# First attention of a two-layer kernel: one stream over all turns, scores as stacked fp32r products, another distance between scores and transposes

## The chip, the cores and the metric

One NeuronCore of a Trainium2 chip. The metric is the device time of one launch in microseconds (us), the median of the runs. Names: TensorE is PE in the profile, VectorE is DVE, ScalarE is ACT, GpSimd is POOL, and SP is the SyncE queue that issues most of the transfers.

## The reference, cut to what matters

Two layers over 8 sequences of 256 tokens with 256 features. Each is LayerNorm, an attention, a mixture of experts as a gate, and a residual. The change is in the attention of layer 0:

```python
q = heads(hidden_states @ wq.T + bq)      # 32 heads of 8 features
k = heads(hidden_states @ wk.T + bk)
v = heads(hidden_states @ wv.T + bv)
scores = jnp.einsum('bhqd,bhkd->bhqk', q, k) / np.sqrt(HD).astype(np.float32)
scores = jnp.where(causal, scores, -jnp.inf)
attn = jax.nn.softmax(scores, axis=-1)
out = jnp.einsum('bhqk,bhkd->bhqd', attn, v)
return out.transpose(0, 2, 1, 3).reshape(B, S, H) @ wo.T + bo
```

Beside it runs the router of layer 0: `xn @ Wr.T`, a softmax over 8 experts and the best two of each token. After it come the experts' blocks, then layer 1.

## The kernel before, in words

**Turns and slots.** The first attention goes over four turns of 512 tokens, two sequences each (TURNS, CH). A turn has 32 slots (SLOTS), 16 for each of its two sequences (PAIRS, the index bb). A slot is one pair of heads of one sequence; `pair_of` gives its sequence, the half mt of the features, j, and the two groups of 32 partitions in which its heads lie.

**A slot.** `scores` (L624 to L630) makes the causal blocks of 256 queries against 256 keys of both heads, 384 columns a head, one PSUM bank each: an fp32 product of 256 columns (L624), one of 128 (L626), and a bf16 product that adds the mask (L630). Slots alternate between banks 0, 1 and 2, 3, so the scores of slot s wait until the exponentials of s-2 have read them. The keys lie four times in SBUF (`kTm`), each copy masked to one head in four, so that a head is picked out of 32 partitions by zeros. DVE takes the maxima of both heads (L839, L841), ACT the exponentials with their sums (L742, L744), TensorE transposes them (`turn`, L640, three blocks a head, into banks 4 and 5), DVE copies them to SBUF (`copy_probs`, L780), and once in two slots `pv` (L659, L662) multiplies four heads by the values, into bank 6 or 7.

**The order** is written out by hand, one program for each engine, with semaphores. TensorE: scores(s), what stands beside (`beside`), transposes of s-2, and pv. DVE: maxima of s, copies of s-2, beside. ACT: exponentials of s, beside. So LAG = 2 on both TensorE and DVE. Beside the slots run the values (L561), the router's products (L568), the bias row (L575) and the turning of the next turn's normalised tokens (L246), and on DVE the statistics and scaling of the next turn (L216, L226) and the routing (from L357; the ranks are read at L450, the slots finished at L478).

**Between two turns** stand the transposes of the inverse sums (`turn_inverse`, L673), the normalising on DVE (L793), queries and keys of the next turn (`pe_queries_keys`, L550; ACT L710 for queries, DVE L772 for the masked keys, four writes each), and the output projection (`project`, L684) with its DVE add (L799). The scores of a turn start once its queries and keys are ready, at slot 0 (the wait is in `scores`).

**Queues.** SP loads the inputs, constants and all of x, then the first pair's weights of layer 1 (`load_pair(0)`), the shared and routed experts of layer 0, then writes zeros to the rows in DRAM to which tokens are scattered (L2132, eight transfers of up to 2 MB). POOL has the variances of each turn (`pool_all`), then, in the last turn, one scatter of tokens a slot (L502). Once all is scattered, SP loads the first blocks (L2138) and `pe_blocks0` begins (L881).

Of the kernel before, what the change touches and what calls it, by code (L numbers as in the profile page):

```python
# [19 lines left out]
F32 = mybir.dt.float32  # L20
# [24 lines left out]
RING = 3  # L45
LAG = 2
# [57 lines left out]
def build(nc, A, out, phases=3):  # L104
    with ExitStack() as ctx:
# [63 lines left out]
        MASK = cols[:, 0:4]  # L169
        G_NORM = cols[:, 12:13]  # L170
        BQ, BK, BV, BO = (cols[:, 4 + 2 * i:6 + 2 * i] for i in range(4))
# [89 lines left out]
        kTm = carve("attention", HPQ, KC, CH)  # L261
        qT = carve("attention", KC, CH)
# [3 lines left out]
        inv_wide = carve("attention", 2, ST * NH0, HD0)  # L266
        nmax = carve("attention", RING, ST, 2)
        total = carve("attention", 2, ST, NH0)
        inv0 = carve("attention", 2, ST * NH0)
        BLOCKS_AT = SPLIT1 + 2 * 512 + 32  # L270
        assert BLOCKS_AT > 2 * KC * CH + HPQ * KC * CH
# [25 lines left out]
        q_done, k_done, v_done = count("q_done", KC), count("k_done", KC), count("v_done", 2)  # L297
        qT_ready, v_ready = count("qT_ready", KC), count("v_ready", 2 * HPQ)
        keys_ready = count("keys_ready", KC * HPQ)
# [215 lines left out]
        ZERO_PARTS = -(-NB0 // TILES) - (-NB1 // TILES)  # L515
# [10 lines left out]
        ln_stats, ln_mean, ln_rstd = (carve("stay", *n) for n in ((2, 6), (TILES, 2), (TILES, 2)))  # L526
# [7 lines left out]
        def pair_of(s):  # L534

            w = s % PAIRS
            return s // PAIRS, w // (PAIRS // 2), (w % (PAIRS // 2)) // 2, (2 * (w % 2), 2 * (w % 2) + 1)

        def head_of(n):
            bb, mt, j, rows = pair_of(n // 2)  # L540
            return mt * (NH0 // KC) + rows[n % 2] * HPQ + j

        def pe_queries_keys(pe, t, mt):

            xT = norm0.xT
            if mt == 0:
                pe.wait_ge(norm0.xT_ready.sem, norm0.xT_ready.at(t, KC))
            for which, bank, done in ((0, 2 + mt, q_done), (1, 4 + mt, k_done)):
# [3 lines left out]
                last.then_inc(done.sem, 1)  # L552

        def pe_attention0(pe, t):
            xT = norm0.xT
            rows7 = ps[:, 7, :]
# [8 lines left out]
            def logits(turn):  # L565
                for c in range(CT):
                    for kc in range(KC):
                        last = pe.matmul(rows7[:, c * E0:(c + 1) * E0], xT[:, kc, c * P:(c + 1) * P], router0[:, kc, :],  # L568
                                         start=kc == 0, stop=kc == KC - 1)
# [8 lines left out]
            def beside(s):  # L578
# [1909 lines left out]
```

## Time and profile before

| what | value |
|---|---|
| median of 3 runs | 1947.15 us (1938.78 to 1947.18) |
| the profiled execution's own time | 1924.45 us |
| its span | 1922.6 us |
| PE, DVE, ACT, POOL busy | 94%, 67%, 47%, 43% |
| mean granted clock | 0.983 |
| first attention, first scores to the first block's product | 27.1 to 418.8 us |
| chain that ended last, by engine | PE 77%, DVE 10%, POOL 5% |

Busy time is the time in which an engine has an instruction in flight. A timeline row merges neighbouring instructions of one line: its duration reaches to the end of the last, some 0.15 to 0.25 us of which overlaps with the next row on PE. So the distance between starts is what a step costs in the stream. A matmul of fp32 leaves two records.

### The profile page before, as it was taken

How to read it: one execution, taken by the hardware profiler on the slowest of the kernel's cores; microseconds unless marked ns; L12 is line 12 of the kernel's file. 1: busy time of each engine (PE TensorE's matmuls, PEld its weight loads, DVE VectorE, ACT ScalarE, POOL GpSimd, SP SyncE). 2: the span in 40 equal slices, each digit the busy share in tenths (PEclk: the TensorE clock that was granted, in tenths of full speed). 3: DMA queues.
4: the chain of work that ended last, by engine and by line, in shares of the span. 5: the costliest groups of instructions: out<-in, count | busy, mean ns of one | idle time of the engine just before them, and what ended most of it. 6: DMA issues, size and time to landing. Idle time of an engine off the chain costs nothing.

```text
span 1922.6 us, 34586 instructions
## 1 busy us (share of the span) xinstructions
PE 1815.3 (94%) x11822; PEld 1443.5 (75%) x11822; DVE 1282.4 (67%) x2811; ACT 906.2 (47%) x2978; POOL 832.7 (43%) x919
## 2 busy tenths in 40 slices
PE   6999999999987999999999999999999997999986
PEld 4767666767765887788888888888888886777754
DVE  5678787863457788888676766667667664444467
ACT  3657564753433444445454455544545543444422
POOL 2000000320056665565767767777676773000066
PEclk9899999999999999999999999999999998999999
DMA  9600000123342000000000000000000223333344
GB/s 345 231 1 2 1 1 1 59 90 112 90 158 94 1 1 12 1 6 1 15 20 14 19 16 14 19 14 11 25 11 22 77 78 136 106 108 107 105 132 123
DMA packets 75907, 114.29 MB, mean 59 GB/s; under 512 B 9505, under 2 KB 65953, under 8 KB 73089
## 3 DMA queue, kind: packets, MB, share of 16 engines
q1 hardware_dynamic: 66416, 86.38, 13.6%
q0 software_dynamic: 9216, 25.18, 4.0%
q8 instruction: 75, 1.23, 0.3%
q10 hardware_dynamic: 144, 1.05, 0.1%
q14 instruction: 56, 0.45, 0.1%
HBM read 64.86 MB, written 47.71 MB: 59 GB/s over the span
## 4 chain that ended last, share of the span: by engine, by line
PE 77%; DVE 10%; POOL 5%; issue 3%; ACT 3%; DMA 2%; POOLq 0%; DVEq 0%; SPq 0%; ACTq 0%
PE ps L1356 11%; PE ps L1371 9%; PE ps L1443 5%; PE ps L1889 5%; PE ps L1397 4%; PE ps L640 4%; PE ps L624 3%; PE ps L1385 3%; PE ps L1384 3%; PE ps L1383 3%; PE ps L902 2%; POOL work L2084 2%; PE ps L1378 2%; PE ps L1906 2%; PE ps L1908 2%
## 5 line engine op out<-in xcount | busy, mean ns | idle before, releaser
L1356 PE MATMUL ps<-work,weights 128*128 128x256 f32 x1024 | 248.3, 386 | 1.1 <-DVE work L1629 1.1
L1371 PE MATMUL ps<-split 128*128 128x512 f32 x768 | 227.8, 419 | 0.0
L1356 PEld LDWEIGHTS ps<-work,weights 128*128 128x128 f32 x1024 | 186.4, 191 | 22.1 <-DVE work L1629 1.3
L1771 POOL TENSOR_TENSOR work<-work,rope 128x512 f32<-128x512 f32 x128 | 164.5, 1286 | 53.1 <-ACT work L1544 53.0
L1777 POOL TENSOR_TENSOR work<-work 128x512 f32<-128x512 f32 x128 | 164.4, 1284 | 5.0
L502 POOL DMA_INDIRECT xg<-work x96 | 96.9, 1009 | 153.1 <-PE ps L630 140.2
L2084 POOL DMA_INDIRECT work<-yg,work x64 | 62.4, 975 | 227.1 <-DMA yg<-work 207.3
L742 ACT ACTIVATE work<-ps,work 128x128 f32<-128x128 f32 x256 | 95.4, 373 | 124.3 <-DVE work L841 117.4
L1371 PEld LDWEIGHTS ps<-split 128*128 128x128 f32 x768 | 130.9, 190 | 24.6
L780 DVE COPY work<-ps 128x384 f32<-128x384 f32 x256 | 130.0, 549 | 8.5 <-PE ps L640 8.4
L1443 PE MATMUL ps<-weights,work 128*128 128x256 f32 x512 | 124.0, 386 | 2.5 <-ACT work L1600 2.5
L640 PE MATMUL ps<-ident,work 128*128 128x128 f32 x768 | 116.5, 283 | 8.1 <-DVE work L780 8.0
L1651 DVE TENSOR_TENSOR work<-ps,keep_w 128x384 f32<-128x384 f32 x128 | 65.4, 553 | 87.1 <-PE ps L1379 86.8
L744 ACT ACTIVATE work<-ps,work 128x256 f32<-128x256 f32 x256 | 122.4, 478 | 0.0
L2021 DVE SCALAR_TENSOR_TENSOR work<-work,ps 128x176 f32<-128x176 f32 (+1 forms) x95 | 35.0, 369 | 121.5 <-ACT work L1972 121.5
L1585 ACT ACTIVATE work<-ps,work 128x128 f32<-128x128 f32 x256 | 90.6, 366 | 51.4 <-PE ps L1385 51.1
L1443 PEld LDWEIGHTS ps<-weights,work 128*128 128x128 f32 x512 | 99.4, 195 | 16.8 <-ACT work L1600 3.1
L1664 DVE RECIPROCAL work<-ps 128x256 f32<-128x256 f32 x64 | 111.9, 1748 | 0.0
L1550 ACT COPY work<-ps 128x256 f32<-128x256 f32 x128 | 47.1, 368 | 130.3 <-PE ps L1371 130.3
L1889 PE MATMUL ps<-weights,work 128*128 x316 | 106.8, 461 | 0.2 <-ACT work L1966 0.2
L1383 PE MATMUL ps<-work 128*128 128x64 f32 (+1 forms) x512 | 97.3, 272 | 9.1 <-DVE work L1651 9.1
L640 PEld LDWEIGHTS ps<-ident,work 128*128 128x128 f32 x768 | 88.1, 145 | 22.8 <-issue 11.5
(236 smaller groups left out, 4508.8 us busy)
## 6 DMA issues: line engine op xcount, KB each, us to landing
work<-xg SPq DMA_DIRECT2D x118, 128.0 KB, 2.2
yg<-work SPq DMA_DIRECT2D x118, 128.0 KB, 1.7
xg<-work SPq DMA_DIRECT2D x6, 2048.0 KB, 17.8
weights<-in_w SPq DMA_DIRECT2D x8, 1024.0 KB, 9.4
weights<-in_f SPq DMA_DIRECT2D x8, 1024.0 KB, 5.1
weights<-in_f SPq DMA_DIRECT2D x1, 4864.0 KB, 16.0
work<-xn SPq DMA_DIRECT2D x32, 128.0 KB, 2.2
weights<-in_wo SPq DMA_DIRECT2D x1, 2048.0 KB, 8.6
```

What stands on the lines that cost most here:

```text
L640: last = pe.transpose(ps[:, 4 + hh, k * P:(k + 1) * P], prob[:, s % RING, hh, k * P:(k + 1) * P], ident[:, :])
L744: act.activation(pr[:, P:BLK], sc[:, 0:SEQ], ACT.Exp, bias=nmax[:, s % RING, 1, hh:hh + 1], accum_out=total[:, bb, 1, h:h + 1]).then_inc(e ...
L780: dve.tensor_copy(probT[:, s % RINGT, hh, :], ps[:, 4 + hh, 0:BLK]).then_inc(probT_ready.sem, 1)
L1356: last = pe.matmul(ps[:, 2, which * SEQ:(which + 1) * SEQ], w1(h, (which * KC + kc) * P, P), xT[:, kc, :], start=kc == 0, stop=kc == KC - 1)
L1371: last = pe.matmul(ps[:, 3, :], x1_split[:, xp, kc, c * P:(c + 1) * P], w_vg[:, n % 2, wp, kc, :], start=i == 0, stop=i == KC * len(TERMS) ...
L1383: pe.matmul(outs[0], left[:, 0:P], rhs[0], start=True, stop=True)
L1443: last = pe.matmul(ps[:, 7, c * D:(c + 1) * D], ogT[:, hh, c * P:(c + 1) * P], weights[:, W1O + h * D:W1O + (h + 1) * D], start=h == 0 and ...
L1664: dve.reciprocal(enz[:, n % 2, :, :].rearrange("p c n -> p (c n)"), ps[:, 0, SEQ:2 * SEQ])\
L1771: pool.tensor_tensor(qk[:, h % 4, :, :], raw[:, h % 2, :, :], rope[:, 0, :].unsqueeze(1).broadcast_to([P, 2, SEQ]), ALU.mult).then_inc(rot ...
L1777: pool.tensor_tensor(qk[:, h % 4, :, :], qk[:, h % 4, :, :], rot_s[:, h % 2, :, :], ALU.add)\
L1889: last = pe.matmul(ps[:, 2 + b % 2, 0:GUW], xb4T[:, b % 2, kc * P:(kc + 1) * P], experts1[:, bass.ds(offset[b] + kc * GUW, GUW)], start=kc ...
L2084: pool.indirect_dma_start(out=yk4[:, c % 2, k, :], out_offset=None, in_=yg1[:, :], in_offset=bass.IndirectOffsetOnAxis(ap=route1.index[:, ...
```

## The change

- **One stream.** The four turns become one run of 128 slots (ALL), numbered g. What stood between the turns stands beside the slots: inverses and output projection of the first sequence at slots 22 and 24, of the second at 6 and 8 of the next turn; the four projections of the next turn at 16, 18 (18, 20 in the routed turn), 28 and 30; values at 10 and 26. All these are even slots; pv stands in odd ones.
- **Distances.** `LAG, BACK = 3, 2`: TensorE transposes g-3 in slot g, DVE copies g-2 in slot g. The ring of exponentials grows to 4.
- **Stacked scores.** Queries and keys are split into an fp32r upper part and the rest (`split_heads`, on DVE for turn 0, on POOL for the others) and written to DRAM with SP's queue (`write_halves`, 4 transfers of 256 KB a projection); from there stacks of 32 partitions a head are loaded (`load_stack`, 256 KB for two slots, a ring of 5): every pair of halves (a, b) of 8 features. One fp32r product over 32 partitions then gives the whole score. The masked keys (L772) go; weights wq and wk are laid out by heads on the host.
- **SP's order.** The zeros go in 15 parts between stack loads, the experts' weights in parts in turn 2, then the shared ones and the first pair.
- **Routing.** Its DVE steps are spread over more slots; ranks and slots are worked out at slots 2 and 4 of turn 3.

The diff, cut to its core:

```diff
-RING = 3
-LAG = 2
+RING = 4
+LAG, BACK = 3, 2
+FIRST = 16, 18
+ALL = TURNS * SLOTS
+RINGQ = 5
...
+        def split_heads(eng, t, n):
...
+            eng.wait_ge(full_ready.sem, full_ready.at(t, n + 1))
+            if index >= 2:
+                eng.wait_ge(halves_written[ring], 16 * 4 * (index // 2))
+            eng.tensor_copy(halves[:, ring, 0, :], full[:, ring, :]).then_inc(upper_ready.sem, 1)
+            eng.wait_ge(upper_ready.sem, upper_ready.at(t, n + 1))
+            eng.tensor_tensor(halves[:, ring, 1, :], full[:, ring, :], halves[:, ring, 0, :], ALU.subtract).then_inc(lower_ready.sem, 1)
...
+            def lower_bank(t, s):
+                if s == 0 and 0 < t < TURNS - 1:
+                    pe.wait_ge(full_ready.sem, full_ready.at(t, PROJ))
+                    logits(6)
+                if s == 2 and t == TURNS - 1:
...
+                    route0.pe_rank(pe, 6)
+                if s == 22 and t < TURNS:
+                    turn_inverse(t, 0)
+                if s == 24 and t < TURNS:
+                    project(t, 0)
+                if t < TURNS - 1:
+                    if s == 26:
+                        pe.wait_ge(s0_ready.sem, s0_ready.at(t, 1))
+                        values(0)
+                    if s == 28:
...
+                        heads(t + 1, 2, 6)
+                    if s == 30:
...
+                        heads(t + 1, 3, 6)
...
             def scores(g):
...
+                if g % 2 == 0:
+                    pe.wait_ge(stack_loaded[n % RINGQ], 16 * (n // RINGQ + 1))
+                if g >= 2:
+                    pe.wait_ge(exp_done.sem, exp_done.at(0, 2 * g - 2))
+                heads = [(2 * (g % 2) + hh, stack[32 * r:32 * r + 32, n % RINGQ, 0, :], stack[32 * r:32 * r + 32, n % RINGQ, 1, :])
...
+            for g in range(ALL + 9):
+                t, s = divmod(g, SLOTS)
+                if g < ALL:
+                    scores(g)
+                lower_bank(t, s)
+                upper_bank(t, s)
                 for hh in range(2):
-                    if LAG <= s < SLOTS + LAG:
-                        turn(s - LAG, hh)
-                if s > LAG and (s - LAG) % 2 == 0:
-                    pv(s - LAG - 2)
-            turn_inverse(0)
...
-                pe_queries_keys(pe, t + 1, 1)
-            project(0)
-            project(1)
+                    if LAG <= g < ALL + LAG:
+                        turn(g - LAG, hh)
+                if LAG < g <= ALL + LAG and (g - LAG) % 2 == 0:
+                    pv(g - LAG - 2)
...
+            for g in range(ALL + 9):
+                if g < ALL:
+                    largest(g)
+                if BACK <= g < ALL + BACK:
+                    copy_probs(g - BACK)
+                beside(*divmod(g, SLOTS))
...
+            def load_stack(n):
...
+                for w in range(2):
+                    sp.wait_ge(halves_written[w], 16 * 4 * (t * KC + mt + 1))
+                if n >= RINGQ:
+                    sp.wait_ge(scores_done.sem, scores_done.at(0, 4 * (n - RINGQ) + 4))
...
+            for n in range(PROJ):
+                write_halves(0, n)
+                if n == 1:
+                    for i in range(HPQ):
+                        load_stack(i)
+            for i in range(HPQ, RINGQ):
+                load_stack(i)
+            for n in range(RINGQ, TURNS * STACKS):
+                t, i = divmod(n, STACKS)
+                if t < TURNS - 1 and i == 14:
+                    write_halves(t + 1, 0)
+                    write_halves(t + 1, 1)
+                if t and i == HPQ:
+                    write_halves(t, 2)
+                    write_halves(t, 3)
+                load_stack(n)
+                if 0 <= n - RINGQ - 2 < ZERO_PARTS:
+                    zero_rows(n - RINGQ - 2)
+                if t == 2 and i < E0:
+                    load_expert(i)
```

## Rows read from the trace of the kernel before

**Rows 1.** The page's row of busy times, whole span.
```profile
PE 1815.3 (94%) x11822; PEld 1443.5 (75%) x11822; DVE 1282.4 (67%) x2811; ACT 906.2 (47%) x2978; POOL 832.7 (43%) x919
```

**Rows 2.** Windows: us; PE, PEld, DVE, ACT, POOL busy; PEclk; DMA share; GB/s.
```profile
27.10:38.90 11.80, 11.42 (x87) 9.32 (x88) 9.91 (x24) 7.58 (x39) 1.22 (x2) 1.00 0.97 384
38.90:52.60 13.70, 13.70 (x84) 9.65 (x84) 8.02 (x18) 5.43 (x26) 0.00 (x0) 0.50 1.08 380
133.80:230.00 96.20, 92.02 (x855) 66.21 (x856) 75.09 (x158) 59.69 (x271) 1.21 (x2) 1.00 0.01 2
```

**Rows 3.** Timeline of TensorE, 84 to 96: start, us, engine, line, operation, count.
```profile
87.57 0.70 PE L624 MATMUL ps<-work 32*128 32x256 f32 x4
88.66 0.82 PE L640 MATMUL ps<-ident,work 128*128 128x128 f32 x6
91.43 0.64 PE L659 MATMUL ps<-work,weights 128*32 128x256 f32 x8
92.21 0.70 PE L624 MATMUL ps<-work 32*128 32x256 f32 x4
```

**Rows 4.** Timeline of DVE, same stretch.
```profile
88.89 0.42 DVE L839 TENSOR_REDUCE work<-ps 128x2 f32<-128x256 f32 x1
89.82 1.01 DVE L780 COPY work<-ps 128x384 f32<-128x384 f32 x2
90.75 0.42 DVE L839 TENSOR_REDUCE work<-ps 128x2 f32<-128x256 f32 x1
```

**Rows 5.** Timeline of ACT, same stretch.
```profile
90.00 0.37 ACT L742 ACTIVATE work<-ps,work 128x128 f32<-128x128 f32 x1 [1.06 <-DVE work L841]
```

**Rows 6.** Timeline of all engines, 114 to 150.
```profile
118.22 0.98 PE L640 MATMUL ps<-ident,work 128*128 128x128 f32 x6 [1.02 <-DVE work L780]
118.78 1.02 DVE L780 COPY work<-ps 128x384 f32<-128x384 f32 x2 [0.24 <-PE ps L640]
138.48 0.37 ACT L742 ACTIVATE work<-ps,work 128x128 f32<-128x128 f32 x1 [9.01 <-DVE work L841]
140.26 0.70 PE L624 MATMUL ps<-work 32*128 32x256 f32 x4 [0.53 <-ACT work L744]
```

**Rows 7.** Timeline of TensorE, 640.5 to 644: fp32r products of the second attention.
```profile
642.56 0.48 PE L1340 MATMUL ps<-split,tri_r 128*128 128x256 f32 x2
642.87 0.33 PE L1343 MATMUL ps<-split,ones_r 128*128 128x128 f32 x2
```

**Rows 8.** Timeline, 114 to 150: products between two turns.
```profile
122.99 3.60 PE L550 MATMUL ps<-work,weights 128*128 128x512 f32 x8
130.30 3.62 PE L684 MATMUL ps<-weights,work 128*128 128x256 f32 x16
```

**Rows 9.** Timeline, 0 to 48: products beside the first slots.
```profile
28.20 1.89 PE L561 MATMUL ps<-weights,work 128*128 128x256 f32 x8
36.29 1.85 PE L568 MATMUL ps<-router,work 128*128 128x8 f32 x16
```

**Rows 10.** Timeline: first projection read, first and last scores, first block.
```profile
22.07 0.69 ACT L710 ACTIVATE work<-ps,bqs 128x512 f32<-128x512 f32 x1 [2.75 <-PE ps L550]
27.11 0.70 PE L624 MATMUL ps<-work 32*128 32x256 f32 x4
...
406.65 0.70 PE L624 MATMUL ps<-work 32*128 32x256 f32 x4
418.83 0.60 PE L881 MATMUL ps<-ident,work 128*128 128x128 f32 x4
```

**Rows 11.** DMA issues: 256 KB from SBUF to DRAM, last number us to landing.
```profile
xn<-work SPq DMA_DIRECT2D x8, 256.0 KB, 2.1
```

**Rows 12.** Timeline of DVE: statistics, then first and last of twelve slot steps.
```profile
139.29 1.40 DVE L216 BATCH_NORM_STATS2 work<-x_res 128x6 f32<-128x256 f32 x4
...
296.57 0.29 DVE L450 COPY work<-ps 128x136 f32<-128x136 f32 x1
299.85 0.18 DVE L478 CAST work<-work 128x32 int32<-128x32 f32 x1
```

More of the change, by code:

```diff
@@ L257, in build @@
         eps_row, eps_dk, zeros = minus_half[:, 16:32], minus_half[:, 32:32 + ST * 2], minus_half[:, 48:49]
-        kTm = carve("attention", HPQ, KC, CH)
-        qT = carve("attention", KC, CH)
+        stack = part(0, RINGQ, 2, SEQ)
+        halves = part(RINGQ * 2 * SEQ, 2, 2, CH)
+        FULL_AT = RINGQ * 2 * SEQ + 4 * CH
+        full = work[:, FULL_AT:FULL_AT + 2 * CH].rearrange("p (a n) -> p a n", a=2)
+        assert FULL_AT + 2 * CH <= SPLIT1
+        used["attention"] = SPLIT1
         oT0 = carve("attention", KC, CH)
@@ new lines, in act_heads, with act_attention0, values @@
+        def act_heads(act, t, n, bank):
+            which, mt = n % 2, n // 2
+            index = t * PROJ + n
+            act.wait_ge(proj_done.sem, proj_done.at(t, n + 1))
+            if index >= 2:
+                act.wait_ge(lower_ready.sem, lower_ready.at(0, index - 1))
+            act.activation(full[:, n % 2, :], ps[:, bank, :], ACT.Identity, bias=(bqs, BK)[which][:, mt:mt + 1],
+                           scale=(HD0 ** -0.5, 1.0)[which]).then_inc(full_ready.sem, 1)
+        def act_attention0(act):
+            def values(t, c):
@@ new lines, in act_attention0, with dve_attention0, copy_probs, inverse @@
+            values(0, 0)
+            for g in range(ALL + 5):
+                if g < ALL:
+                    exponentials(g)
+                beside(*divmod(g, SLOTS))
+        def dve_attention0(dve):
+            def copy_probs(g):
+                for hh in range(2):
+                    dve.wait_ge(prob_turned.sem, prob_turned.at(0, 2 * g + hh + 1))
+                    if g >= RINGT:
+                        dve.wait_ge(pv_done.sem, pv_done.at(0, 2 * (g - RINGT) + hh + 1))
+                    dve.tensor_copy(probT[:, g % RINGT, hh, :], ps[:, 4 + hh, 0:BLK]).then_inc(probT_ready.sem, 1)
+            def inverse(t, bb):
@@ new lines, in _, with zero_rows, load_expert @@
+            zeros_to = [(rows, b0, min(b0 + ZB, blocks)) for rows, blocks in ((xg0, NB0), (xg1, NB1)) for b0 in range(0, blocks, ZB)]
+            def zero_rows(n):
+                if n == 0:
+                    sp.wait_ge(s_zeroed, 1)
+                rows, b0, b1 = zeros_to[n]
+                sp.dma_start(rows[b0 * P:b1 * P, :].rearrange("(b p) d -> p b d", p=P), S[:, ZB:ZB + b1 - b0, :])\
+                  .then_inc(xg_zeroed, 16)
+            def load_expert(e):
+                if e == 0:
+                    sp.wait_ge(s2_lower, 1)
+                    sp.wait_ge(bias_done, 6)
+                at = W0F + e * EW
+                sp.dma_start(weights[:, at:at + EW], A["f0"][:, e * EW:(e + 1) * EW]).then_inc(f0_loaded, 16)
@@ L2230, in _ @@
                 norm0.pool_all(pool, t)
+                for n in range(PROJ):
+                    split_heads(pool, t, n)
             pool.wait_ge(xg_zeroed, 16 * ZERO_PARTS)
@@ L2269, in _ @@
             dve.tensor_copy(bias_wide, BV.unsqueeze(2).broadcast_to([P, KC, P])).then_inc(bias_ready0, 1)
+            for n in range(PROJ):
+                split_heads(dve, 0, n)
             dve.wait_ge(consts_loaded, NCONST)
```

493 lines of the change are left out of this document (244 added, 249 removed).

## Prediction

> **What bounds the kernel now.** I read the page first: TensorE is busy 94% of the span [rows 1]. Then I cut the span into stages with the view of windows. The change touches only what runs from the start to the last projection of the first attention, some 420 of 1922.6 us; in a whole turn (133.8 to 230.0) TensorE is busy 92 of 96 us, DVE 75, ACT 60 [rows 2]. Third, the timelines of single engines inside a turn, because the busy share doesn't say who waits for whom. Two slots take 4.64 us on TensorE (87.57 to 92.21) with no gap: scores and masks 1.09 (87.57 to 88.66), the six transposes 0.75 to 0.9, and once in two slots the product by values, 0.78 (91.43 to 92.21) [rows 3]. So the slot, 2.32 us, is TensorE's own work. DVE needs 1.86 for a slot: 0.93 for the two maxima (88.89 to 89.82) and 0.93 for the two copies (to 90.75) [rows 4].
>
> **The new score products.** An fp32 product leaves two records of two passes; before, a slot has 4 records of 256 columns and 4 of 128. With fp32r it has 2 and 2, one pass each. The rows have fp32r products of 256 columns every 0.155 us (two in 642.56 to 642.87), so there is no fourfold pass left [rows 7]. The two heads run side by side in different rows of the array. From two passes twice to one pass once, 256 and 128 columns at 2.4 GHz, 0.48 us goes, and 0.61 is left from the first score product to the first transpose. Upper bound 1.09 (nothing gained), lower bound 0.35 (masks and one weight load); I take 0.61, next to the 0.67 that the fp32r row would give.
>
> **The new order, which is the point.** In slot g TensorE now issues scores(g), then what stands beside, then the transposes of g-3. DVE in slot g does the maxima of g, then the copies of g-2. So the copies that DVE does in its slot g-1 are those of g-3, and their transposes stand behind scores(g) on TensorE. Scores(g) have to wait for the exponentials of g-2, whose two PSUM banks they reuse. That closes a loop of two slots, and each hop has a row:
> - maxima start to exponentials start: 1.11 (88.89 to 90.00) [rows 4, 5];
> - exponentials start to the next scores in those banks: 1.78 (138.48 to 140.26) [rows 6];
> - scores to transposes: 0.61;
> - transposes to the first copy: 0.56 (118.22 to 118.78) [rows 6];
> - two copies, then the maxima of g: 0.93 [rows 4].
> Sum 4.99 us for two slots, 2.50 for one, against 2.32 now. Before, transposes of s-2 stood in slot s on both engines, so the same loop took three slots: with the old scores 5.47/3 = 1.82, hidden under TensorE's 2.32. The change takes 0.48 us from TensorE per slot (its own work would be about 1.84), and puts a wait in its place: TensorE idles some 0.65 and DVE some 0.63 in each slot. From the first scores (27.11) to those of slot 127 (406.65) it is 379.5 us now [rows 10]. After, 63.5 pairs x 4.99 = 317.
>
> **What stands beside, on TensorE.** It stands between scores(g) and the transposes, so inside the loop, and always in even slots, so always in the same of the two interleaved chains: nothing of it falls into the idle time. A projection of 512 columns costs 1.8 (8 records, two calls, 3.60) and an output projection 1.8 (16 records, two calls, 3.62) [rows 8]; the four transposes of an inverse 0.5, as four of a slot's six (0.82 with their tail) [rows 3]; half the values 1.8 (1.89), the router's products 1.8 (1.85) [rows 9]. Turn 0: router 1.8, bias row 0.9, values 1.8, turning x 1.0 (as the inverses, twice), four projections 7.2, inverse 0.5, output 1.8, values of the next 1.8: 16.8. Turn 1: the same without bias, with the inverse and output left from turn 0: 18.2. Turn 2: once more the router, 20.0. Turn 3: ranking (no row alone; 0.7, of little weight), two inverses, two outputs, one values: 7.1. Sum 62.
>
> **Beside, on DVE.** Steps in odd slots lengthen the same chain: statistics and scaling at slots 3 and 7, 1.4 each [rows 12], three turns, 8.4; eleven small routing steps in odd slots of turn 2 at 0.29 (twelve take 3.46, 296.57 to 300.03) [rows 12], 3.2. In even slots they fall on the other chain, which has 4.99 - 2 x 1.86 = 1.27 to spare: inverses (1.0), normalising and output copies (0.7) are hidden there, and would cost up to 19 us in all (two of each a turn) if the loop were shorter. The slots' computation in slot 2 of turn 3, 3.5 behind an inverse of 1.0, sticks out by 3.2. Sum 14.8. Gone are the masked keys, eight DVE writes a turn between the turns.
>
> So first to last scores: 317 + 62 + 14.8 = 394, 14 more than now. The seams between turns, where the old kernel drains, are worth little, since they are filled with projections (122.99 and 130.30 in [rows 8]): in a turn of 96 us, 32 slots x 2.32 = 74, beside 6.7, and the seam's products 11.6 leave 3.7 of waiting.
>
> **Start, end, and what moves to other queues.** The first scores wait for a way through DRAM: projection, ACT, two DVE steps (the first projection is there at 22.07 [rows 10]; ACT 0.7 and two DVE steps of some 0.6 bring it to about 24.0), four writes of 256 KB on SP's queue, the same for the keys, then a load of 256 KB. A transfer of this size takes 2.1 us to land [rows 11], the engines moved 384 GB/s [rows 2], so 2 MB need 5.5: halves there at about 30.3, first stack at 32.9, first scores at 33.0 instead of 27.11. +6 (bounds +3, if the writes overlap wholly, and +12, if each waits in turn). Later writes and stacks (16 MB each way over 400 us, 80 GB/s) have four stacks, 20 us, of lead: free; if not, a load is 2 to 5 us on the path of a stack. The zeros, weights of the experts and of the first pair leave the first 75 us and go out between stack loads; they are needed after turn 2 or later: free. POOL splits 12 projections, two steps each, where it idled: free. The end: now 12.2 us from the last scores to the first product of the blocks (406.65 to 418.83) [rows 10]; after, half the inverse and output work is already done, but the chain scores, maxima, exponentials, transposes, copies, values, output remains: -1.
>
> **The clock.** In turn 0 it is granted at 1.2 GHz from 38.9 to 52.6, after 11.8 us with the router's 8-column products and gaps, though TensorE counted as busy for 11.4 of them [rows 2]. The changed kernel idles before the first scores and in every slot, and issues the router's products four times in the stream. I add 6 us (estimate; bounds 0 and, as a rival, far more).
>
> Sum: +14 + 6 - 1 + 6 = **+25 us**. The profiled execution took 1924.45 around a span of 1922.6, 22.7 under the median 1947.15; +25 makes it 1949.5, and the median, against which I predict, 1972. With 0.35 or 1.09 for the scores the pairs give -17 or +30 on that; with the other bounds the forecast's own range is +8 to +45. About 0.5%, 9.7 us, is what a measurement can tell from no change.
>
> **Rivals.**
> 1. *The loop is shorter than I say, and the change is faster.* If copies of g-2 don't have to wait behind scores(g+1), the slot is bounded by work: DVE 1.87, TensorE 1.84, and products beside fall partly into idle time. Then 128 x 1.87 + 62 + 15 = 316, times 1.04 for waits like those at the seams, 329 instead of 380: with the start, -45 us, 1902. A weaker form: the slot is 2.50, but half of the 62 us hides: 1941. It decides from a slot period under 2.3 on. For it: before, TensorE alone set the pace, so no row shows my loop binding. Against: each hop is a semaphore wait in the code, with a row for its length. 0.27, the weak form 0.05 of it.
> 2. *The clock falls for long.* TensorE's work per slot sinks by a fifth and its period grows, with a gap in every slot, and in turn 0 the clock fell behind a stretch with gaps. At 1.2 GHz two old slots cost between 7.8 (84 records in 13.7 us, 24 to a slot [rows 2]) and 9.3 (twice 4.64); less 2 x 0.96 for the scores 5.9 to 7.4, say 6.2. If half the stage runs so: 32 pairs x 1.2, and 31 us of the beside work a second time: +69 on the forecast, 2041. Against: in turn 1 the granted clock was 1.00 over 96 us with gaps at the seam [rows 2]. The Trainium skill, TensorE: Matmul & The Clock Gate, section Part 4: PE-mode transpose, says that transposes do not count as busy in the way other matmuls do; six of them make up a third of a slot now and would make up as much after, with the score products shorter; by that rule this case comes true, with 2041. Turn 1's row speaks against it, with the same transposes at full clock, and no run yet shows the changed mix. 0.10.
> 3. *Cancelled.* Loop as forecast, but start, clock and part of the beside work cheaper, 1947 within 10 us. 0.10.
>
> **How the numbers follow.** Forecast 0.53. Faster by over 0.5%: rival 1 without its weak form, 0.22. Within 0.5%: the weak form and rival 3, 0.15. Slower: forecast and rival 2, 0.63. Range 1918 to 2015: it holds the forecast with its bounds (0.53), rival 3 and the weak form (0.15), the milder halves of rival 1 (a partly shorter loop) and of rival 2 (0.11 and 0.05), some 0.84 before allowing for what I have not thought of; left out are rival 1 in full and a clock down for half of the stage.
>
> **What would show it.** Right: in a plain stretch maxima every 2.50 us; DVE idle about 0.6 before the copies, released by the transposes; TensorE idle before the first score product, released by ACT; score groups about 0.6 long; first scores at about 33; a turn of about 100 us. Wrong: a period under 2.3, DVE idle at the maxima instead of the copies, products beside that don't lengthen their slot, or windows with a granted clock near 0.5 in turns 1 to 3.

## The result, and the profile after

The changed kernel takes 2010.68 us (median of 4 runs, 2010.25 to 2016.34); the kernel before takes 1944.04 on the same chip (4 runs, 1938.78 to 1947.18). The ratio is 1.035 (95% interval 1.032 to 1.039): 66.6 us slower. The prediction was slower by 25, with 1918 to 2015 as its range. The sign is right, and so are the loop that was forecast and most terms, but more than half of the loss is missing.

The page of the changed kernel, with the groups that answer to [rows 1] and to the steps of the sum:

```profile
PE 1790.1 (89%) x11310; PEld 1425.4 (71%) x11310; DVE 1268.3 (63%) x2787; ACT 906.5 (45%) x2986; POOL 855.8 (43%) x943
...
q8 instruction: 107, 1.75, 0.4%
...
L827 DVE COPY work<-ps 128x384 f32<-128x384 f32 x256 | 131.8, 552 | 135.8 <-PE ps L705 130.0
...
L810 ACT ACTIVATE work<-ps,work 128x128 f32<-128x128 f32 x256 | 95.4, 373 | 182.5 <-DVE work L907 169.4
...
L689 PE MATMUL ps<-split 32*128 32x256 f32 x256 | 53.0, 404 | 101.3 <-ACT work L812 93.4
...
L705 PE MATMUL ps<-ident,work 128*128 128x128 f32 x768 | 116.5, 291 | 0.7 <-DVE work L827 0.7
```

The three waits of the forecast loop are among the costliest: DVE's copies (L827) wait for the transposes (L705), ACT's exponentials (L810) for the maxima (L907), and TensorE's scores (L689) for the exponentials (L812). The transposes hardly wait for the copies, 0.7 us in all. TensorE did less (1790 us busy against 1815) in more time.

Where the stage's time lies, by the timeline of the changed kernel: first and last maxima, and the first product of the blocks.

```profile
36.99 0.42 DVE L905 TENSOR_REDUCE work<-ps 128x2 f32<-128x256 f32 x1 [2.17 <-PE ps L695]
...
452.66 0.41 DVE L905 TENSOR_REDUCE work<-ps 128x2 f32<-128x256 f32 x1
...
464.36 0.85 PE L937 MATMUL ps<-ident,work 128*128 128x128 f32 x3
```

First and last maxima of the kernel before:

```profile
30.11 0.41 DVE L839 TENSOR_REDUCE work<-ps 128x2 f32<-128x256 f32 x1
...
407.93 0.42 DVE L839 TENSOR_REDUCE work<-ps 128x2 f32<-128x256 f32 x1 [0.81 <-PE ps L630]
```

The first product of the blocks stands at 418.83 there [rows 10]. So the start costs 6.9 us more, the stream takes 415.7 where it took 377.8, and the end 11.7 for 10.9. Together 45.5 us are lost by the first product of the blocks. Another 20 are lost in a part that the diff doesn't touch, the second attention (experiments on TensorE's places).

The two profiles lie further apart than the medians, 86.2 us (spans of 2008.8 and 1922.6), and the rest of it isn't the change's. From the last product of L1951 (L1889 in the kernel before) to the end, the changed kernel's profile takes 119.3 us and that of the kernel before 101.4. Both lengths occur whatever the kernel: 100 to 102 us in the profiles of the first four experiments and of three later ones, 115 to 121 in four, among them the kernel before with nothing but waits added (116.5). Of each chip with more than one profile, all showed the same of the two. What decides between them stays open; a ratio of two kernels on one chip should be free of it.

**The loop, hop by hop.** Timeline of the changed kernel in a plain pair of slots, DVE, ACT and TensorE:

```profile
402.01 1.02 DVE L827 COPY work<-ps 128x384 f32<-128x384 f32 x2 [1.23 <-PE ps L705]
...
402.95 0.41 DVE L905 TENSOR_REDUCE work<-ps 128x2 f32<-128x256 f32 x1
403.06 0.38 PE L689 MATMUL ps<-split 32*128 32x256 f32 x2 [0.76 <-ACT work L812]
...
403.66 0.82 PE L705 MATMUL ps<-ident,work 128*128 128x128 f32 x6
...
404.05 0.37 ACT L810 ACTIVATE work<-ps,work 128x128 f32<-128x128 f32 x1 [1.05 <-DVE work L907]
404.19 1.02 DVE L827 COPY work<-ps 128x384 f32<-128x384 f32 x2 [0.23 <-issue]
...
405.92 0.39 PE L689 MATMUL ps<-split 32*128 32x256 f32 x2 [0.65 <-ACT work L812]
...
406.52 0.82 PE L705 MATMUL ps<-ident,work 128*128 128x128 f32 x6
```

Maxima to exponentials 1.10 (402.95 to 404.05), exponentials to the next scores in those banks 1.87 (to 405.92), scores to transposes 0.60 (to 406.52), transposes to copies 0.53 (403.66 to 404.19), copies to maxima 0.94 (402.01 to 402.95): 5.04 us for two slots. Forecast were 1.11, 1.78, 0.61, 0.56 and 0.93, 4.99 in all.

**A pair with a product beside.** Timeline of TensorE in the changed kernel, turn 3, with an output projection (L612, two calls):

```profile
387.33 0.39 PE L689 MATMUL ps<-split 32*128 32x256 f32 x2 [1.43 <-ACT work L812]
...
387.94 1.89 PE L612 MATMUL ps<-weights,work 128*128 128x256 f32 x8
389.67 0.82 PE L705 MATMUL ps<-ident,work 128*128 128x128 f32 x6
...
394.11 0.38 PE L689 MATMUL ps<-split 32*128 32x256 f32 x2 [1.44 <-ACT work L812]
```

From 387.33 to 394.11 are 6.78 us, 5.04 and the 1.73 of the product (387.94 to 389.67). TensorE stands still for 1.43 us before the scores in the same pair, and the product does not go there, since its place in the order is inside the loop.

**The clock.** Windows by turn (columns as in [rows 2]), first the changed kernel, then turn 0 of the kernel before:

```profile
37.00:143.70 106.70, 82.63 (x687) 60.45 (x687) 65.26 (x142) 59.35 (x272) 13.96 (x13) 0.88 0.68 224
143.70:249.40 105.70, 82.53 (x725) 59.80 (x721) 68.81 (x151) 59.73 (x273) 8.71 (x10) 0.92 0.38 123
249.40:361.10 111.70, 84.84 (x718) 61.47 (x716) 73.59 (x168) 60.24 (x275) 8.33 (x10) 0.90 0.35 113
361.10:452.70 91.60, 66.97 (x677) 49.25 (x677) 68.30 (x150) 54.14 (x253) 31.30 (x33) 0.94 0.28 92
```

```profile
30.10:137.40 107.30, 105.00 (x875) 75.73 (x876) 75.56 (x159) 59.72 (x272) 1.22 (x2) 0.89 0.48 167
```

A mean of 0.92 over 105.7 us is 17 us at 1.2 GHz and the rest at 2.4. All four turns give 26, 17, 22 and 11: some 76 us at half clock. The kernel before had some 24 in turn 0 and under 5 after it.

### The profile page after: what moved, and what is told of

Its sections match the earlier page's. It is cut to its first block, busy times and chain, and to the rows that moved or that the text cites. A ratio compares the mean times of both kernels' runs of the same rounds, so it can differ in the third digit from the quotient of the medians.

```text
span 2008.8 us, 34162 instructions
## 1 busy us (share of the span) xinstructions
PE 1790.1 (89%) x11310; PEld 1425.4 (71%) x11310; DVE 1268.3 (63%) x2787; ACT 906.5 (45%) x2986; POOL 855.8 (43%) x943
## 4 chain that ended last, share of the span: by engine, by line
PE 68%; DVE 13%; ACT 7%; issue 6%; POOL 3%; DMA 2%; another core or an unknown queue 1%; SPq 0%; DVEq 0%; ACTq 0%; POOLq 0%
PE ps L1418 11%; PE ps L1433 7%; PE ps L1505 5%; PE ps L1951 5%; PE ps L1459 4%; ACT work L812 3%; PE ps L1447 3%; PE ps L1446 3%; PE ps L1445 3%; PE ps L958 2%; ACT work L810 2%; PE ps L705 2%; DVE work L907 2%; PE ps L1440 2%; PE ps L1968 2%
## 5 line engine op out<-in xcount | busy, mean ns | idle before, releaser
L827 DVE COPY work<-ps 128x384 f32<-128x384 f32 x256 | 131.8, 552 | 135.8 <-PE ps L705 130.0
L810 ACT ACTIVATE work<-ps,work 128x128 f32<-128x128 f32 x256 | 95.4, 373 | 182.5 <-DVE work L907 169.4
L689 PE MATMUL ps<-split 32*128 32x256 f32 x256 | 53.0, 404 | 101.3 <-ACT work L812 93.4
L812 ACT ACTIVATE work<-ps,work 128x256 f32<-128x256 f32 x256 | 122.5, 479 | 0.0
L689 PEld LDWEIGHTS ps<-split 32*128 32x128 f32 x256 | 27.2, 196 | 131.3 <-issue 97.3
L705 PE MATMUL ps<-ident,work 128*128 128x128 f32 x768 | 116.5, 291 | 0.7 <-DVE work L827 0.7
L1459 PE MATMUL ps<-work 64*128 64x256 f32 (+1 forms) x1024 | 104.3, 345 | 12.9 <-issue 11.3
L562 POOL CAST split<-work 128x512 fp32r<-128x512 f32 x12 | 7.3, 610 | 250.9 <-ACT work L755 250.9
```

Of the source, the lines that this page charges most:

```text
L705: last = pe.transpose(ps[:, 4 + hh, k * P:(k + 1) * P], prob[:, g % RING, hh, k * P:(k + 1) * P], ident[:, :])
L810: act.activation(pr[:, 0:P], sc[:, SEQ:BLK], ACT.Exp, bias=nmax[:, g % RING, 0, hh:hh + 1], accum_out=total[:, bb, 0, h:h + 1])
L812: act.activation(pr[:, P:BLK], sc[:, 0:SEQ], ACT.Exp, bias=nmax[:, g % RING, 1, hh:hh + 1], accum_out=total[:, bb, 1, h:h + 1]).then_inc(e ...
L827: dve.tensor_copy(probT[:, g % RINGT, hh, :], ps[:, 4 + hh, 0:BLK]).then_inc(probT_ready.sem, 1)
L1459: last = pe.matmul(ps[:, 4 + hh, at], k[rows, half, keys], q[rows, half, queries], start=half == 0, stop=half == 1)
```

## The experiments

The edits are against the changed kernel, except where the kernel before is named. Ratios are with the kernel before, measured on the same chip; where times are compared stage by stage, it is by the first and last maxima of each profile.

### DVE's copies three slots back

```diff
-LAG, BACK = 3, 2
+LAG, BACK = 3, 3
```

> The changed kernel with one number altered: BACK = 3, so DVE copies in slot g the probabilities of g-3, which TensorE transposes in the same slot. Theory (copy loop): the loop scores, transposes, copies, maxima, exponentials, scores then spans three slots again and no longer binds; what is left is the loop of the two PSUM banks, 0.61 + 0.23 + 1.11 + 1.78 = 3.73 us for two slots, and DVE's 3.74. Two plain slots take about 3.8 us instead of the 5.04 measured; first to last maxima 415.7 us falls to about 320, the time to about 1915. Rival (stack loads come late, or the clock is what slows the stage): two plain slots stay at about 5, the time stays within 20 us of 2010.

Measured: 1890.03 us, ratio 0.982 (0.980 to 0.985), where the change alone has 1.035. The stream takes 316.9 us (37.32 to 354.19) for 415.7. The timeline of DVE in a pair:

```profile
168.92 0.41 DVE L905 TENSOR_REDUCE work<-ps 128x2 f32<-128x256 f32 x1
...
170.78 0.41 DVE L905 TENSOR_REDUCE work<-ps 128x2 f32<-128x256 f32 x1
...
173.04 0.42 DVE L905 TENSOR_REDUCE work<-ps 128x2 f32<-128x256 f32 x1 [0.33 <-PE ps L695]
```

Two slots take 4.12 us (168.92 to 173.04), 1.86 of DVE's own work and 2.26 with one short wait for the score products; 3.8 were expected. The constant BACK alone opens the loop: DVE copies g-3 in slot g, the same slot in which TensorE transposes it, so the way from scores to copies, maxima, exponentials and back to scores spans three slots. So the wait of the prediction's sum is shown, and the idea of the change (stacked scores, one stream) is worth having without it.

### The old distance on both engines

```diff
-LAG, BACK = 3, 2
+LAG, BACK = 2, 2
```

> The changed kernel with LAG, BACK = 2, 2: both engines work two slots behind, as before the change; the product by values now falls in even slots, beside the other products. Theory (copy loop): as with BACK = 3, about 3.8 us for two plain slots; two slots with 1.8 us of products beside and the product by values together cost more on TensorE, so the stage takes 320 to 335, the time 1915 to 1930. Rival (scores far ahead are what saves time and the loss lies elsewhere): slower than the changed kernel, over 2015.

Measured: 1888.66 us, ratio 0.981 (0.979 to 0.984). The stream takes 319.5 us (37.37 to 356.87). It is not how far ahead the scores are that costs, nor how near: it is the difference of LAG and BACK. Equal distances, 2 or 3, give the same time within 2 us.

### Scores as fp32 products of the same stacks

```diff
-                heads = [(2 * (g % 2) + hh, stack[32 * r:32 * r + 32, n % RINGQ, 0, :], stack[32 * r:32 * r + 32, n % RINGQ, 1, :])
+                heads = [(2 * (g % 2) + hh, stack[32 * r:32 * r + 32, n % RINGQ, 0, :].bitcast(F32), stack[32 * r:32 * r + 32, n % RINGQ, 1, :].bitcast(F32))
```

> The changed kernel with the score products of the stacks in fp32 instead of fp32r: same order, same data, four passes. Theory (the score products are a hop of a loop of two slots): 0.48 us is added to each pair, 64 pairs, +31 us: time about 2041, two plain slots 5.5 us. Rival (TensorE has idle time in each slot, so the products' length doesn't matter): within 5 us of 2010. The stage alone at 5.5 against 4.64 of the old kernel would say what the new distances cost without the gain of fp32r.

Measured: 2020.13 us, ratio 1.049 (1.046 to 1.052); the stream takes 454.3 us (38.16 to 492.44), 38.6 more than with fp32r. A plain pair is 5.52, so 0.48 longer, as the loop theory wants of a term that stands in it once a pair: 64 pairs give 31. The other 8 I put down to the clock, which in one window of this kernel is far down (windows as above); no run shows that share by itself:

```profile
150.00:200.00 50.00, 45.08 (x308) 33.32 (x307) 27.71 (x64) 18.68 (x89) 1.81 (x3) 0.69 0.29 93
```

So the fp32r product is worth what was said, 0.48 us, where it stands on the path.

### Products beside put behind the transposes

```diff
-                lower_bank(t, s)
-                upper_bank(t, s)
                 for hh in range(2):
                     if LAG <= g < ALL + LAG:
                         turn(g - LAG, hh)
                 if LAG < g <= ALL + LAG and (g - LAG) % 2 == 0:
                     pv(g - LAG - 2)
+                lower_bank(t, s)
+                upper_bank(t, s)
```

> The changed kernel with what stands beside on TensorE moved behind the transposes of its slot, ahead of the product by values. Theory: now the 62 us beside are in the loop between the scores and the transposes and cost all their length. Behind the transposes they delay only the next slot's scores, which have some 0.65 us to spare and pass the rest on: about 20 of 62 us stay, first to last maxima 415.7 falls to about 375, the time to about 1970. Rival (products beside cost their length wherever they stand, or the idle time is not there): within 8 us of 2010.

Measured: 1936.01 us, ratio 1.007 (1.005 to 1.010). The stream takes 366.9 us (37.20 to 404.09), 48.8 less. Most of the 62 us beside were on the path only because they were issued ahead of the transposes; behind them they fall into idle time like the 1.43 us above. The plain pairs stay as they were.

### TensorE's instructions moved by 90 places

The second attention runs in a loop over sequences (a `Fori` from 2 to the last but one) which the change leaves as it was. The timeline of TensorE at its jump back, changed kernel first, then the kernel before (where a last row has fewer than 16 products, it reaches only to the window's end, and its start is what counts):

```profile
1074.29 0.39 PE L1447 MATMUL ps<-work 128*128 128x128 f32 x2
1077.40 2.46 PE L1459 MATMUL ps<-work 64*128 64x256 f32 x16 [2.72 <-issue]
...
1203.60 1.73 PE L1459 MATMUL ps<-work 64*128 64x256 f32 x10 [2.59 <-issue]
```

```profile
1028.21 0.39 PE L1385 MATMUL ps<-work 128*128 128x128 f32 x2
1028.53 1.58 PE L1397 MATMUL ps<-work 64*128 64x256 f32 x16
...
1149.69 1.58 PE L1397 MATMUL ps<-work 64*128 64x256 f32 x16
```

An iteration takes 126.2 us (1077.40 to 1203.60) for 121.2 (1028.53 to 1149.69), and TensorE stands still at the jump, waiting for nothing but its own issue. The stall is one part of the 5.0 us, and a fall of the granted clock behind it the other: L1459 takes 2.46 us for 1.58. In the profile of the kernel with BACK = 3 the clock didn't fall behind one of the jumps (1.00 from 1103 to 1113 us), L1459 takes 1.58 behind it, and the iteration from there takes 124.3 us (1105.64 to 1229.95):

```profile
1105.64 1.58 PE L1459 MATMUL ps<-work 64*128 64x256 f32 x16 [2.58 <-issue]
```

The row of the queue that loads instructions, over 470 us inside the loop of the changed kernel (packets, MB, share):

```profile
q8 instruction: 32, 0.52, 0.4%
```

The kernel before has no such row in its loop; in its whole span it has 75 packets of this queue where the changed one has 107. A packet is 16 KB, and in the straight parts one comes every 256 instructions of TensorE. The edit puts waits that are met at once ahead of TensorE's first work:

```diff
+            for _ in range(180):
+                pe.wait_ge(pow_rows, 1)
```

> The changed kernel with 180 waits that are always met put ahead of TensorE's first work, so that every later TensorE instruction stands 180 places further on; nothing else differs. Theory of instruction loads: TensorE's loop over sequences in the second attention takes 126 us an iteration after the change against 121.2 before, because at each jump back TensorE stands still 2.6 to 3.0 us while instructions are loaded again; whether that happens depends on where the loop starts in the chunks of 256 instructions that are loaded (40 before, 102 after, 26 here). Expected: no loads of TensorE's instructions between the iterations, no stall at the jump, 121 us an iteration, and 20 us less than the changed kernel, about 1.025 of the kernel before (1.035 without the shift). The 180 waits themselves run while the first inputs come in and cost under 3 us. Rival: the loop is longer since something in it waits for another engine or queue; then the iterations stay at 126 us and the ratio at 1.035.

Measured: ratio 1.026 (1.023 to 1.029) for 1.035; q8 is down to 71 packets, none in the loop, and no stall at the jump (timeline of TensorE, the same line):

```profile
1072.64 1.58 PE L1459 MATMUL ps<-work 64*128 64x256 f32 x16
...
1194.27 1.47 PE L1459 MATMUL ps<-work 64*128 64x256 f32 x14
```

An iteration takes 121.6 us. The stream of the first attention is as before (415.4), so the two losses are separate.

### The same on the kernel before, by 30 and by 65 places

```diff
+            for _ in range(60):
+                pe.wait_ge(pow_rows, 1)
```

> The kernel before with 60 waits that are always met put ahead of TensorE's first work, so that its loop starts at place 100 of a chunk of 256 instructions where it started at 40. Theory of instruction loads: the old kernel gets the new one's stall: instructions are loaded again at each jump back, 126 us an iteration instead of 121.2, and 20 us more in all, a ratio of about 1.010. Rival (something of the change itself makes the loop longer): no stall, 121 us an iteration, ratio 1.000.

Measured: ratio 1.001 (0.999 to 1.002), iterations of 121.7 us, no loads in the loop. The expectation fell, but for reasons in the records. 60 waits added 30 instructions, not 60. And the places in the last two expectations (40, 102, 26) were counted from another origin; counted from the loads themselves, the loop starts at place 118 of its chunk in the kernel before and at 180 in the changed one. Hence the next run, with 130 waits:

> The kernel before with 130 waits that are always met. The run with 60 of them showed no loads inside the loop; its records tell why that says nothing yet: two such waits come out as one instruction (1198 semaphore records against 1168), so it moved the loop by 30 places and not by 60. The loads of the straight part come every 256 instructions of TensorE; counted from them the loop of 1636 instructions starts at place 118 in its chunk in the kernel before (it lies in 7 chunks), at 148 with 60 waits (7 chunks), at 180 in the changed kernel (8 chunks), at 14 with its 180 waits (7 chunks). Here it is 183: 8 chunks. Theory: loads in every iteration come back, 9 an iteration, 126 us instead of 121, and 18 to 20 us more in all, a ratio of about 1.010. Rival: the old loop doesn't stall wherever it lies, ratio 1.000.

Measured: 1940.99 us, ratio 1.009 (1.007 to 1.011). The old kernel now has the stall, and the loads (timeline of TensorE, then the queue's row over 470 us in the loop):

```profile
1033.95 2.35 PE L1397 MATMUL ps<-work 64*128 64x256 f32 x14 [3.19 <-issue]
...
1159.94 2.27 PE L1397 MATMUL ps<-work 64*128 64x256 f32 x16 [3.16 <-issue]
```

```profile
q8 instruction: 33, 0.54, 0.5%
```

An iteration is 126.0 us. Nothing of the change is in this kernel, so the place of the loop alone does it. The third run is the control, the changed kernel with 60 waits:

> The changed kernel with 60 waits, 30 instructions: the loop starts at place 210 of its chunk, 8 chunks as without them. Theory: the loads in every iteration and 126 us stay, and so does the ratio of the changed kernel to the one before, 1.035. Rival: it is the waits themselves, or any shift at all, that took the loads away in the run with 180; then 121 us an iteration and a ratio of 1.026.

Measured: ratio 1.034 (1.032 to 1.036), iterations of 126 us. Waits as such don't help. Six placements agree, though the origin of the count was set when four of them were known: a loop of 1636 instructions that starts at place 14, 118 or 148 of its chunk of 256 lies in 7 chunks and stays loaded; at 180, 183 and 210 it lies in 8 and is loaded anew, 9 chunks an iteration. The Trainium skill, Advanced Engine Details and Errata, section ISA Cache, gives 128 KB for TensorE and 16 KB or 256 instructions a line, which would make eight lines (an estimate from its two figures; the section also says "Only 2 cache lines!", and with two a loop in 7 chunks could not have stayed loaded). By eight, 7 chunks and the next one fit and 8 and the next don't. The runs agree with its line size, and with eight lines if one chunk is loaded ahead, which the ninth load an iteration suggests and no run shows.

### Both repairs together, and with the later order

The first kernel has BACK = 3 and the 180 waits, the second has the later order of the products beside as well.

> The projections three slots apart (BACK = 3) and the 180 waits together. Both causes are separate in place, so they should add: 1890.0 less 20 is 1870, a ratio of 0.972 with the kernel before. If the sum is a rival's (the loop's stall is no cause of its own), it stays at 0.982.

> The same as the one with BACK = 3 and the 180 waits, and the beside products (the two banks of the next turn's projections and the like) put behind the transposes of their slot in place of ahead of them. With two slots between the projections this order was worth 50 us, since TensorE's beside products stood in the loop scores, maxima, exponentials, transposes, copies, projections. Theory: with three slots between them that loop no longer sets the pair of slots, TensorE's own work does (4.14 us a pair), and the order is worth nothing: the time stays within 6 us of the one before it. Rival: part of the loop still binds in the pairs with beside products, and a further 10 to 40 us go.

Measured: ratios 0.977 (0.974 to 0.980) and 0.975 (0.972 to 0.977). The stream takes 318.4 us in both (36.94 to 355.31, and 37.69 to 356.12). The order beside is worth 48.8 us while the loop binds and nothing once it doesn't, as expected. The 180 waits bring the ratio from 0.982 to 0.977, about 10 us, where 20 were expected; the iterations of this run are 121.5 us long, so the stall is gone. But 20 were not there to win: with BACK = 3 alone the iterations took 125.4, 124.3, 125.4 and as long again, since the clock fell for less time behind the jumps and behind one of them not at all, and the four together are 14 us longer than in this run. The two ratios come from different chips, each with an interval of 5 us to either side, so 10 can't be told from 14.

### TensorE's idle time filled

```diff
+                if g == 0:
+                    pe.wait_ge(s_zeroed, 1)
...
                               pT[:, 0:SEQ], start=j == 0, stop=False, skip_group_check=True)
+                for _ in range(2):
+                    for r, pT in four:
+                        pe.matmul(ps[r:r + 32, 6 + bb, at:at + SEQ], S[:, TILES - 1, 0:32],
+                                  pT[:, 0:SEQ], start=False, stop=False, skip_group_check=True)
```

The weights (`S`) are zeros by then (the added wait sees to it), so the sums of the product by values stay as they are.

> The changed kernel, in which each product by values is followed by eight more fp32 products of 256 columns in four groups of rows, with zeros as weights, so that nothing is added to its sums. They fall into the 1.43 us in which TensorE stands still before the scores of each even slot, where it waits for ACT; eight should take 0.9 us (four with their weights take 0.45 at full clock). They are 1024 instructions, so TensorE's later loop keeps its place and its stall. Theory of the clock: TensorE's idle time in the slots is what brings its clock down to half in 78 us of the stage; with 0.9 of some 1.3 us of it filled in each pair, less than 40 us at half clock are left, plain pairs stay at 5.0 us, and 8 to 20 us go, a ratio of 1.025 to 1.030 against 1.035. Rival: idle time isn't what decides (the mix of instructions is, or the stops at single waits), then some 78 us at half clock stay and the ratio is 1.035 or up to 1.045, since the added products take longer at half clock. Second rival: the products don't fit and lengthen the pairs, by up to 0.9 us in 64 pairs, a ratio up to 1.06.

Measured: 1987.31 us, ratio 1.033 (1.031 to 1.034). The added products (L730) fit into the wait (timeline of TensorE), and the windows by turn show the clock:

```profile
190.38 1.05 PE L730 MATMUL ps<-work 128*32 128x256 f32 x16
...
192.05 0.38 PE L689 MATMUL ps<-split 32*128 32x256 f32 x2 [0.40 <-ACT work L818]
```

```profile
37.20:145.50 108.30, 94.67 (x915) 66.73 (x916) 65.01 (x142) 59.38 (x272) 13.87 (x13) 0.89 0.66 217
145.50:247.70 102.20, 90.51 (x979) 63.37 (x978) 68.20 (x151) 59.74 (x273) 8.70 (x10) 0.98 0.40 127
247.70:359.10 111.40, 94.66 (x971) 65.86 (x968) 73.18 (x169) 60.26 (x275) 8.39 (x10) 0.94 0.36 118
359.10:450.50 91.40, 77.81 (x917) 55.81 (x921) 67.81 (x150) 53.81 (x250) 31.26 (x33) 0.96 0.29 92
```

In turn 1, TensorE is busy 90.5 us for 82.5, the granted clock rises from 0.92 to 0.98, and the turn takes 102.2 us for 105.7, though it has more to do. In turns 1 to 3 together, the time at half clock falls from some 50 us to 25. But turns 2 and 3 take as long as before (111.4 for 111.7 and 91.4 for 91.6). Less came of it than I expected, since turn 0 keeps its 24 us, and in other slots the added products cost what the clock gave back.

One pair shows the fall itself. It has the half of the values (L580) beside, and TensorE waits 2.73 us ahead of it. Timeline of TensorE in the changed kernel:

```profile
279.10 0.52 PE L689 MATMUL ps<-split 32*128 32x256 f32 x2 [2.73 <-ACT work L812]
280.05 3.16 PE L580 MATMUL ps<-weights,work 128*128 128x256 f32 x8
...
287.49 0.38 PE L689 MATMUL ps<-split 32*128 32x256 f32 x2 [1.43 <-ACT work L812]
```

It takes 8.39 us, 3.4 of them at half clock. With the filling the same pair waits 1.86, stays at full clock, has L580 at 1.89 and takes 6.77. So idle time on TensorE has a part in the lower clock here, and it is not enough for it: in plain pairs of the changed kernel TensorE is busy 29 of 40 us, no more than in any whole turn, and the clock stays up (window as above):

```profile
400.00:440.00 40.00, 28.99 (x304) 21.50 (x304) 30.59 (x64) 26.88 (x127) 14.15 (x15) 1.00 0.27 87
```

The added products also change the mix, with a smaller share of transposes in it. No run holds the mix and changes the idle time alone.

## Why the prediction was right or wrong

**The loop, its length and its reason: right.** 5.04 us for two slots against 4.99, each hop within 0.1. Idle time stands where it was said to stand. Over 63.5 pairs the difference is 3 us. Rival 1 (a shorter loop) has fallen; it comes near to what the kernel does at BACK = 3, with 1.86 and 2.26 us for the two slots where it had 1.87.

**The score products: right.** 0.60 for 0.61, and fp32 in their place costs 0.48 a pair.

**Products beside: right.** The one that was followed, an output projection, adds its whole length to its pair. Putting them behind the transposes took away 48.8 of the 62 us.

**Start and end: a little short, within the bounds given for the start.** The forecast counts from the first scores, and these come 8.6 us later than before, not 6: at 35.73, where 33.0 was said.

```profile
35.73 0.58 PE L689 MATMUL ps<-split 32*128 32x256 f32 x2 [6.22 <-DMA split<-heads_by_part]
```

The transfers of 256 KB took 3.1 and 3.3 us to land (medians of the changed kernel's page) where 2.1 was assumed. From the last scores (450.59) to the blocks it takes 13.8 for 12.2, so +1.6 for -1. In the stream, the stacks, zeros, weights and POOL's splitting cost nothing that can be seen: at BACK = 3 all of them are there, and it takes 316.9 us.

**The clock: mis-sized.** "I add 6 us" is the first step that failed. First to last scores were to be 394 us apart, and 400 with the clock; they are 414.9 (35.73 to 450.59). With 3 us for the longer pairs, some 18 are left for the clock in place of 6. How much of it the clock explains can be estimated from two comparisons of turns. In the kernel before, turn 0 took 107.3 us at a clock of 0.89, and with 60 harmless waits ahead of it 100.0 at 1.00 (window below): 7.3 us for some 24 at half clock. In turn 1, filling took 3.5 us off for some 13 (0.92 to 0.98). At 0.27 to 0.31 for each us at half clock, the 76 us come to 21 to 24. This is an estimate, and a loose one: the pair above lost 1.6 us for 3.4 at half clock, a plain pair can lose nothing (from 249.35 to 254.39 us the first maxima of two slots are the usual 5.04 apart, though 2.5 of them ran at half clock), and turns 2 and 3 got nothing back for some 12. It puts the clock at about the 18 that are left, and the split among the smaller terms stays open. Rival 2 had the direction and put it too high: half of the stage at 1.2 GHz and +69, where 18% of it was. Its argument from idle time holds in part, as the last experiment shows. The rule beside it in the prediction (the Trainium skill, TensorE: Matmul & The Clock Gate, section Part 4: PE-mode transpose), that transposes don't count as busy the same way, doesn't by itself bring the clock down: with BACK = 3 the transposes are the same and the score products as short, and the windows stand at 0.97, 1.00 and 1.00. Whether they count for less where TensorE also idles, no run shows. First the window of turn 0 of the kernel before with 60 waits, then those of BACK = 3:

```profile
30.30:130.30 100.00, 94.66 (x876) 68.60 (x876) 75.20 (x160) 59.61 (x272) 1.22 (x2) 1.00 0.52 180
```

```profile
100.00:150.00 50.00, 47.58 (x443) 33.83 (x436) 42.28 (x95) 35.55 (x164) 4.96 (x6) 0.97 0.68 221
150.00:200.00 50.00, 49.05 (x456) 33.79 (x455) 41.43 (x85) 39.10 (x174) 7.56 (x8) 1.00 0.52 163
200.00:250.00 50.00, 47.58 (x458) 33.34 (x456) 45.23 (x104) 36.40 (x169) 3.08 (x4) 1.00 0.49 168
```

**The part that was left out: instruction loads.** "The change touches only what runs from the start to the last projection of the first attention" is the second step that failed, and by 20 us the larger one. The change makes TensorE's program of the first attention shorter, which moves the loop of the second attention from place 118 of its chunk to place 180. Four jumps back at 5.0 us each (126.2 less 121.2) are 20. The stall itself is 2.7, and the fall of the granted clock behind it costs the rest. The rows that would have told it were there before: the queue of instruction loads silent from 1030 to 1500, and a loop of 1636 instructions. What was forecast for the attention itself, +25, stands against 45.5; with the loop's 20 the total is 65.5, and 66.6 was measured. That these two agree to a microsecond is in part luck: the stage times come from single profiles, and turn 0 alone moved by 7 us between two profiles of the kernel before.

**Chances and range.** The forecast's sign and case came true. Its own range has a sum that doesn't fit: with 1.09 for the scores, 30 us more than forecast, the upper end is +55 and not +45. The attention's part, 45.5, lies about there; the whole, 66.6, lies above both. The wider range, to 2015, held the median of 2010.68 because it had been opened for a clock that falls for longer, while 20 us of the loss came from a loop that the prediction left out. That is luck.

## What to carry to other kernels

When two engines work on a ring at distances of their own, write down which slot's instruction stands behind which on each engine, and close the loop. Here one slot between LAG = 3 and BACK = 2 made a loop of two slots out of one of three and cost 99 us, with what it did to the clock. Work beside such a loop belongs behind its last link; ahead of it, it costs its full length with idle time next to it. And a change of a program's length ahead of a hardware loop can move that loop so that it lies in one chunk of instructions more: count the loads inside the loop before and after, and shift it with a few harmless instructions if they appear.

## What the runs showed of the hardware that I had not expected

- TensorE's loop of 1636 instructions costs 121.2 to 121.7 us an iteration in 7 chunks of 256 instructions and 124 to 126 in 8, with 9 loads of 16 KB in each. The stall at the jump is 2.6 to 3.2 us; whether the granted clock falls behind it makes the difference between 124 and 126.
- TensorE's clock fell behind a wait of 2.73 us, and stayed at 1.00 over 40 us in which it was busy for 29. Its mean busy share doesn't tell the clock.
- Two waits on the same semaphore in a row came out as one instruction (180 waits, 90 records; 60 waits, 30).
- The same kernel before had a median of 1944 us on the first chip, 1941 on another and 1923 to 1924 on two. So times of different chips are compared only as ratios. The last 100 us of the program took 15 to 20 us more on some chips, with either kernel.
- Turn 0 of the kernel before took 107.3 us in one profile, with 24 us at half clock, and 100.0 in another with 60 waits ahead of it, with none, though the waits didn't change the time of the whole measurably (1.001). Some of the loss at half clock in a single profile may be chance.
